# A four-layer graph network on one core: the edge layer's gathered blocks replaced by sorted ones

## What is computed

```python
x = layernorm(x + L0(x))     # mean of x[src] per dst; concat(x, mean) @ W.T + b
x = layernorm(x + L1(x, w))  # two hops of a w-weighted, degree-normalised sum; mean of x and the hops
x = layernorm(x + L2(x, e))  # segment_sum(relu(concat(x[src], x[dst], e) @ W1 + b1) @ W2 + b2, dst)
x = layernorm(x + L3(x))     # two SAGE layers (mean @ W_l + b + x @ W_r), a relu between
```

## Time and profile before

| | us |
|---|---|
| runs: median of three | 3688.67 |
| runs: lowest, highest | 3682.96, 3693.33 |
| the profiled execution: span | 4015.9 |
| its engines, busy: PE, DVE, POOL, ACT | 3290.8, 2244.4, 1153.0, 1011.7 |
| start and histogram | 0 to 275 |
| build | 275 to 1195 |
| L0 | 1195 to 1262 |
| weights passes L1A, L1B | 1262 to 2150 |
| edge layer L2 | 2150 to 3552 |
| counts passes L3A, L3B | 3552 to 4016 |

### The profile page before, as it was taken

The page is one execution under the profiler, slowest core; times in us unless marked ns, Lnnn a source line. Parts: engine busy times, 40 slices in busy tenths (PEclk is TensorE's granted clock), DMA queues, the critical chain, the costliest instruction groups (busy, mean ns, idle before and its releaser), DMA issues.

```text
span 4015.9 us, 126981 instructions
## 1 busy us (share of the span) xinstructions
PE 3290.8 (82%) x56384; PEld 3021.5 (75%) x56384; DVE 2244.4 (56%) x3103; ACT 1011.7 (25%) x2184; POOL 1153.0 (29%) x1012
## 2 busy tenths in 40 slices
PE   0768999999997888888886577777787777789998
PEld 0757999999996888888885466665566565689898
DVE  8974777666767767677776234444454444331122
ACT  0025777777771000000000111111111111110000
POOL 5587000000001000001001665565566555501100
PEclk9987999999997999999997677777778777799999
DMA  4315777777776999988885343343344433369798
GB/s 122 98 38 179 280 282 278 269 275 269 282 284 242 381 394 381 382 362 345 344 357 192 83 108 107 102 113 104 100 117 109 114 100 104 99 275 343 297 372 326
DMA packets 285688, 904.33 MB, mean 225 GB/s; under 512 B 97944, under 2 KB 162702, under 8 KB 256850
## 3 DMA queue, kind: packets, MB, share of 16 engines
q1 hardware_dynamic: 235802, 857.37, 55.4%
q0 software_dynamic: 35520, 36.44, 6.7%
q10 hardware_dynamic: 13832, 2.70, 0.4%
HBM read 644.17 MB, written 252.83 MB: 223 GB/s over the span
## 4 chain that ended last, share of the span: by engine, by line
PE 39%; issue 35%; DVE 9%; DMA 6%; POOL 4%; another core or an unknown queue 2%; POOLq 2%; DVEq 2%; SPq 1%; ACT 0%; ACTq 0%
PE ps L1601 10%; PE ps L1418 7%; PE ps L1413 5%; DMA stream<-a_weights 5%; PE ps L1632 4%; PE ps L1596 4%; PE ps L1635 4%; PE ps L1521 2%; POOL wend L909 2%; POOL stream L916 2%; DVE operand_room L2274 1%; DVE junk L1739 1%; DVE operand_room L2291 1%; DVEq L2299 1%
## 5 line engine op out<-in xcount | busy, mean ns | idle before, releaser
L936 POOL DMA_INDIRECT stream<-table,stream x660 | 794.4, 1204 | 544.9 <-PE ps L1601 322.6
L1370 PE MATMUL ps<-operand_room 64*128 64x50 bf16 (+1 forms) x18750 | 645.6, 222 | 50.4 <-issue 18.1
L1370 PEld LDWEIGHTS ps<-operand_room 64*128 64x128 bf16 x18750 | 618.9, 163 | 81.8 <-issue 29.6
L1418 PE MATMUL ps<-stream,node_room 125*64 125x125 f32 x10000 | 579.2, 277 | 60.2 <-DMA stream<-a_weights 51.1
L1418 PEld LDWEIGHTS ps<-stream,node_room 125*64 125x64 f32 x10000 | 557.2, 140 | 70.9 <-DMA stream<-a_weights 57.5
L1074 ACT CAST stream<-ps 128x500 bf16<-128x500 f32 (+2 forms) x700 | 431.0, 632 | 246.1 <-PE ps L1370 193.2
L1074 ACT COPY stream<-ps 128x500 f32<-128x500 f32 (+2 forms) x700 | 421.5, 618 | 0.0
L1215 ACT ACTIVATE node_room<-ps 128x320 f32<-128x320 f32 x300 | 131.3, 438 | 885.7 <-remote 460.3
L1413 PE MATMUL ps<-operand_room,stream 125*125 125x192 bf16 x3750 | 319.2, 247 | 4.4 <-POOLq L578 4.4
L1413 PEld LDWEIGHTS ps<-operand_room,stream 125*125 125x125 bf16 x3750 | 313.5, 137 | 4.7 <-POOLq L578 4.7
L2356 DVE TENSOR_TENSOR node_room<-slot_f,stream 128x625 f32<-128x625 f32 x240 | 184.1, 809 | 210.9 <-remote 177.6
(11 more groups left out here) (292 smaller groups left out, 4518.3 us busy)
## 6 DMA issues: line engine op xcount, KB each, us to landing
stream<-a_weights SPq DMA_DIRECT2D x100, 3125.0 KB, 15.0
a_weights<-stream SPq DMA_DIRECT2D x500, 312.5 KB
stream<-a_counts SPq DMA_DIRECT2D x100, 1562.5 KB, 9.1
a_counts<-stream SPq DMA_DIRECT2D x500, 156.2 KB
stream<-sorted_edges SPq DMA_DIRECT2D x80, 781.2 KB
node_room<-sorted_edges SPq DMA_DIRECT2D x40, 781.2 KB
stream<-dst_run SPq DMA_DIRECT2D x20, 1031.2 KB
stream<-table,stream POOLq DMA_INDIRECT x660
```

The costliest lines, as they stand in the source:

```text
L936: pool.indirect_dma_start(emsg[s][:, t, :], None, tables[L2][:, :], bass.IndirectOffsetOnAxis(src_t[j % 3][:, at:at + 1], 0))\
L1370: ins = pe.matmul(out if step == 0 else out[:, 1:2], low[s][rows_a, :, t], planes[s][rows_a, t // TI, what, :, t % TI], start=step == 0, s ...
L1418: ins = pe.matmul(ps_sum[SUM_BANK[MATRIX[k]][b]][half:half + D, 0:Q], tab_in_of(k)[0:Q, h, :], a[0:Q, h, :], start=h < 2, stop=h >= NPP - 2)
```

## The change

- All 50 blocks are sorted and go by units; the gathers, the table in DRAM, `src_run`, `e_rows`, the split of e and the 60 chunks with their gathered part are gone. `NB` rises from 40 to 51.
- 50 sorts lie beside the weights passes, one per two dense blocks (`sort_with`), with `hot_src`, `hot_pair` and `run_rank` in two buffers. `sort_tables` and the first pairs move ahead of L0.
- The small steps that make keys and values move from DVE to GpSimd (`sort_values`), two sorts ahead; the three remaining parts on DVE are `sort_pairs`, `sort_counts` (with `fold`) and `sort_vals`.
- The edge layer has 100 chunks of half a block, five units each, 500 units. A chunk's load brings 6400 columns in bf16 to 125 partitions, in two DMAs of 112 and 13 rows, three buffers deep. DVE makes one compare of 6400 columns and the slot one-hots of 25 slots in bf16; GpSimd widens units 0, 2 and 4 of each chunk to f32, ACT units 1 and 3.
- The piece splits of L3A go to GpSimd but for the last group's; two blocks of counts are loaded before the edge layer ends.

```diff
-    PE_BLOCKS = [g * GT + POG + i for g in range(GROUPS) for i in range(PEG)]
-    POOL_BLOCKS = [g * GT + i for g in range(GROUPS) for i in range(POG)]
+    NPE = NPP
+    NCH = 2 * NPP
+    HRING = 3
+    POOL_SLOTS, ACT_SLOTS = (0, 2, 4), (1, 3)
+    EVEN_Q = P - 16
...
-            def gather_runs():
...
-                    for t in range(CHUNK):
-                        at = c % CPB * CHUNK + t
-                        pool.indirect_dma_start(emsg[s][:, t, :], None, tables[L2][:, :],
...
+            def sort_values(b):
+                pool.wait_ge(sort_in[b % 2], 48 * (b // 2 + 1))
...
+                pool.tensor_scalar(run_tmp[0][:, 0:TILES], run_dst[b % 2][:, 0:TILES], float(1 - b * Q), None, ALU.add)
+                pool.tensor_scalar(vals[:, :, 1, :], pairs(pack[:, :, 1]), 1.0, None, ALU.add)
+                pool.tensor_copy(vals[:, :, 2, :], e_of)
+                pool.drain()
...
+                pool.sem_inc(vals_rdy, 1)
...
+            def sort_with(n):
+                s = n // 2
+                if n % 2:
+                    sort_vals(s, 0)
+                    if s + 1 < NPE:
+                        sort_counts(s + 1)
+                else:
+                    if n:
+                        sort_vals(s - 1, 1)
+                    else:
+                        sort_counts(0)
+                    if s + 1 < NPE:
+                        sort_pairs(s + 1)
...
+                for lo, hi in ((0, EVEN_Q), (EVEN_Q, Q)):
+                    sp.dma_start(to[lo:hi, :], rows_of[0:HW].partition_broadcast(hi - lo)).then_inc(unit_in[c % HRING], 16)
...
+                        for n in POOL_SLOTS:
+                            if c:
+                                pool.wait_ge(unit_done, UPC * (c - 1) + n + 1)
+                            pool.tensor_copy(unit_slot[n], slot_hot[c % 2][:, n * SUB:(n + 1) * SUB, 0:Q])
```

More of the change, by code:

```diff
@@ L522, in build_program @@
         LINEAR = {"linear": (L0, L1A, L1B, L3A, L3B), "gather": ()}
[L523 removed]
+        TO_DRAM = {"linear": (), "gather": (L0, L1A, L1B, L2, L3A)}
         def count(users, k, g):
@@ L1571, in weights_pass @@
-                    dense(k, g, odd if g % 2 else even)
+                    dense(k, g, between)
                 turn_sums, *nodes = node_steps(k, GROUPS - 1, "linear")
```

943 lines of the change are left out of this document (387 added, 556 removed).

## The result

The changed kernel has 3834.8 us (median of four runs, 3826.5 to 3846.2) beside 3687.8 us for the kernel before: a ratio of 1.0405, 95% interval 1.0381 to 1.0429. It is slower by 147 us. The forecast was slower, 3760 us, in a range of 3540 to 3890: the direction and the range held, but the loss is twice the 71 us forecast.

The account below looks back on a forecast made before the run. The prediction took an ordinary edge layer to go at the gathers' pace, and DVE to bound the weights passes after the change. 3689 + 190 − 120 + 5 = 3764 us, taken as 3760, range 3540 to 3890.

Parts of the forecast that it names:

- DVE becomes the bound of the weights passes: Weights passes: 1020 us of DVE work plus 16 and 40, about 1076 us against 888, +190 us.
- the 40 us: Weights passes: GpSimd's small sort operations cost DVE 0.8 us a sort, 40 us in 50 sorts.
- The 30% of the earlier trace: From 272 to 295 us, beside busy GpSimd, DVE's L1982 took 1820 ns against a median of 1401, 30% longer.
- The ordinary edge layer of before: Edge layer before: all 327 us by which the profile exceeded the runs lie there, leaving 1075 us of 1402.
- rival 1: Edge layer before: TensorE's starved stretches are in every run, so the change wins, total 3450 to 3640 us; chance 0.28.
- The gathers' pace as the bound of that stage: Edge layer before: 660 gathers on GpSimd at 1.484 us each, 980 us in all, set an ordinary run's pace.
- 26 + 895 + 12 + 14 = 947 us: Edge layer after: 26 us to the first unit, 500 units at 1.79 us, products 12 us, tail 14 us.
- the helpers' part: Edge layer after: per chunk DVE 4.0, ScalarE 3.6, GpSimd 2.7 us, all under 8.95; loads of 4.4 us hidden.
- The sign that the prediction named: Edge layer after: its term would be wrong if units took over 2.1 us or waited for loads.
- 3689 + 190 − 120 + 5 = 3764: Whole kernel: median before, weights passes +190 us, edge layer −120, wider histogram compares +5.
- stray waits: Edge layer: allowance for which the gain of 128 us was counted as only 120.

Follow-up runs that it names:

- short-loads run: Kernel before with its broadcast loads cut into pieces of at most seven slots, the same bytes: 3698.3 us beside 3684.0.
- even loads: Kernel before with each broadcast load in two transfers of 112 and 13 rows: 3626.1 us beside 3684.1, ratio 0.9863.
- eighths: Changed kernel with each broadcast load of the edge layer cut by columns into eight parts, nothing else: 3734.7 us beside a before of 4009.

## Why the prediction was right and wrong

- *DVE becomes the bound of the weights passes: right.* The sum had 1020 us of DVE work, 16 of waits for TensorE and 40 for GpSimd, 1076; the stage has 1048. The work per sort was 18.6 for 18.45, and the waits for TensorE 30 us. The term that failed is the 40 us: GpSimd's small operations cost nothing that shows (1044 against 1045 us). The 30% of the earlier trace rows was read beside GpSimd operations of over 1 us each (20.58 us in 18) and did not carry over to these; whether their length is the reason was not tested. The rule of the Trainium skill, "SBUF — State Buffer", section "SBUF: two separate sides", agrees with the trace as to the lock, 3.72 us for an operation that takes 0.26 us at its shortest; the one who paid was GpSimd, which has time.
- *The ordinary edge layer of before, 1402 − 327 = 1075 us: near in size, wrong in cause, so its size was luck.* It is some 1100 (1110 in the short-loads run, which is 14 us slower than before). The excess was not the profiler's: three more profiles agree with their runs at 4002 to 4015 us. Beside a before of 4002 us the change would most likely have come out faster, with the sign of rival 1. That stalls of TensorE under the gathers make the difference was right: with one gather per chunk they go.
- *The gathers' pace as the bound of that stage: right as a pace (980 us forecast, 983 with even loads), but not the only bound.* Loads of 125 rows stood beside it; even loads alone gave 75 us, from 1066 to 991.
- *The edge layer after, 26 + 895 + 12 + 14 = 947 us: wrong, and the step that failed.* Measured were 1090. The units' price of 1.79 us was right, and both ends were near, 33 and 11 us for 26 and 14. What failed is the multiplication: 500 × 1.79 supposes that instructions arrive. In the helpers' part I asked whether the loads are in time for DVE, and took them as hidden; they were in time, TensorE waited 11 us in all for a compare. But in packets of 12.8 KB they held up TensorE's instructions: pauses of 114 us, and a lower clock after them. From first to last unit the 500 units and the products took 1049 us where the sum had 895 + 12 = 907; without the loads they take 908, in eighths 913, and the whole stage 957. The sign that the prediction named, units of over 2.1 us, would have passed it by: the median unit had 1.78 us, and the mean came to 2.10.
- *The sum.* Forecast 3689 + 190 − 120 + 5 = 3764, measured 3835. The weights passes were 28 us cheaper, and of the edge layer's gain of 120 us only 20 came: the stage after was 143 us over its 947, the stage before 35 over its 1075, and 8 had been kept for stray waits. The two terms missed in opposite directions, so the total hides 28 of the edge layer's 100. Without the pauses the change would have about 3714 us (an estimate from the eighths), still over before's 3688, and the forecast of 3760 would have been 46 too high.

Open is what decides the level. The two are not the kernel before's alone: the build takes 888 to 893 us in every kernel at the first and 897 to 924 us at the second, with TensorE's pauses beside the 50 gathers there. The rest of the changed kernel, without a gather, is as long at both. So at the slower level gathers hold TensorE up and at the faster one they don't; why, no run shows. No run combined all 50 sorted blocks with a shorter chain on DVE that worked; the eighths alone (3735) win against a before of 4009 by 6.7% (0.9328, 0.9305 to 0.9352), and were not measured beside one of 3684 us, to which they would lose by some 1% as things stand.

## What to carry to other kernels

When a stage's sum is "instructions times duration" for an engine with a long unrolled program, look at its "issue" gaps beside the landings of the instruction queue. If it has them, cut large broadcast loads into short packets: it changed a few lines here and gave 136 us in the stage (1049 to 913), about 120 of the total. Where there were no such gaps, it gave nothing (before with short loads). Split a load of 125 rows into 112 and 13. And before an excess of a profile is put down to the profiler, profile the same kernel again: it may have two levels.

## What the runs showed of the hardware

- Broadcast loads can hold up TensorE's instructions. Beside 12.8 KB packets at a DMA share of 0.59 a 16 KB instruction packet took 1.39 us and TensorE had 59 "issue" pauses; beside 3.2 KB packets 1.15 us and 12, beside 1.6 KB packets of the same bytes 0.98 us and one, without the loads 1.09 us and none. The weights passes, with packets of 25 KB at a share of 0.77, have 0.98 us and no such pause; the program advances more slowly there (115 instruction packets in 1045 us against 160 in 1049).
- A broadcast to 125 partitions moves 1.6 MB in 13.3 us at a DMA share of 0.32; in two transfers of 112 and 13 rows the same load keeps up with chunks of 9.1 us.
- GpSimd operations of 33 columns that start beside a long DVE operation with two inputs end with it (0.26 us at the shortest, 3.72 beside a scan); DVE does not show a loss to them (1045 and 1044 us).
- A reduction of 1700 bf16 columns over the outer dimension takes 3325 ns on DVE, twice the 1.7 us of a product of that size.
- An indirect DMA of 128 rows costs GpSimd 1.49 us in the mean, 1.19 busy and 0.30 of "issue".
- The kernel with 660 indirect DMAs had two levels, 3684 and 4002 to 4014 us, each held for a whole series; with 100 of them and even loads they are 58 us apart (3473 and 3531). At the slower level TensorE has "issue" pauses beside gathers (7 to 20 beside the 50 of the build, 376 to 428 beside the 660), at the faster one none in the build and one or six in an edge layer with all of them.
